# A fused attention and FFN layer on one core: a third PSUM bank for the projections, another order of GpSimd's work, and v turned by VectorE and a trip through DRAM

## The chip, the cores and the metric

The kernel runs on 1 core of one Trainium2 chip. The time is the device time of one execution in microseconds; a kernel's time is the median of its runs.

## The reference

The input has 2048 rows (8 sequences of 256 tokens) of 512 numbers. First attention with 32 heads of 128, grouped over 8 key/value heads, then a linear layer whose rows are switched on by clusters, each behind a layer norm and each added to its input:

```python
NH, NKV, D = (32, 8, 128)
qkv = layernorm(x) @ w_qkv                       # 512 -> 6144
scores = einsum('bqhgd,bkhd->bhgqk', q, k) * D ** -0.5
bias = where(rel >= 0, -slopes * sqrt(rel), -inf)  # causal
attn = softmax(scores + bias)
x = x + (attn @ v) @ w_o                         # 4096 -> 512
dots = softmax(layernorm(x) @ centroids.T / 0.1)
hits = dots > 0.01
dense = layernorm(x) @ weight.T + bias
x = x + where(any(hits, 1)[:, None] & any(hits, 0)[assignments], dense, 0)
```

## The kernel before

**Tiles and units.** The rows are cut into 4 quads of 512 tokens (two sequences each). A unit `u` of the main loop is one key/value head with its 4 query heads for one quad; there are 32 units, four quads for each of 8 head groups `g`. A unit does six projections (`project(u, i)`: k, then four heads of q, then v), the scores of 4 heads, a softmax, the product with v and the output product with w_o. It is pipelined over two units: in `body(u)` unit u is projected and scored while the probabilities of unit u-1 are applied to v (`apply_v`, six chunks) and pass through w_o (`project_out`, four tiles).

**Precision.** Every operand of TensorE is split in a high and a low float32r part, and a product is three matmuls (high·high, high·low, low·high: `three_pass`). So each result in PSUM is read twice: ScalarE copies it out as the high part, VectorE (or GpSimd, when the source lies in SBUF) writes what is left as the low part.

**Causal halves.** For the first 128 queries of a sequence (`qt == 0`) only 128 keys count. There `scores` multiplies the high part of q with the 256 columns `both` (k high and k low side by side), then the low part of q with the same 256 columns, and `add_bias` on VectorE adds the two halves.

**Turning.** The probabilities are turned for `apply_v` in two steps: VectorE turns 32x32 blocks into `ring_whole`, then SyncE's queue writes the chunk to the DRAM tensor `turned` and reads it back with the blocks rearranged (`turn_out`, `turn_in`). ScalarE makes `pT_hi` of it, GpSimd the low part (`pT_lo_part`, in place in `ring`). v is turned by TensorE: ScalarE copies the projection to `vT` in SBUF, TensorE transposes four 128x128 blocks (L1294), ScalarE writes `v_hi`, VectorE `v_lo`.

**Order.** Each engine's program is written out by hand, in order, with semaphores between the engines. The places that matter here:
- The projections alternate between the two PSUM banks `PJ`; project(u, i) waits until VectorE has read projection i-2 for its low part (`qk_lo_done`, L807 for q, L804 for k).
- GpSimd splits the next group's w_qkv at the end of every fourth unit (`split_qkv`, four chunks, each with the DMA issues of a later load behind it, `load_after`) and then opens `wqkv_ready`. It splits w_o in the second unit of a group between chunks of the probabilities (`split_o`, in `group`) and opens `wo_ready`, for which `project_out(u, 0)` waits.
- Units 0 to 3 also carry the layer norm of the next quad; units 30 and 31 the FFN's first work; what follows unit 31 is written out by hand.

## Time and profile before

| | |
|---|---|
| median of 3 runs | 1324.68 us (1323.49 to 1326.9) |
| the profiled execution, own time | 1328.74 us |
| its span in the trace | 1327.1 us |
| granted TensorE clock, mean over the span | 0.992 of full speed |
| busy: TensorE 96%, VectorE 72%, ScalarE 47%, GpSimd 36% | |

The span is the time from the first instruction in the trace to the last. A matmul's bar in the trace is longer than the distance to the next one, since matmuls overlap; how fast TensorE goes is read from the distance between starts.

### The profile page before, as it was taken

The numbers are of one execution on the slowest core, as the hardware profiler recorded it, in microseconds if no ns is written. First come the engines' busy times: TensorE is split into PE (matmuls) and PEld (weight loads), VectorE is DVE, ScalarE is ACT, GpSimd is POOL, SyncE is SP. The second block draws the span as 40 slices with busy tenths as digits, with TensorE's granted clock in tenths as the row PEclk, the third lists the DMA queues.
The fourth block names the chain that finished last, engine by engine and source line by source line (L and its number), as shares of the span: only waits on it lengthen the run. The fifth ranks groups of instructions, "written<-read, shape, count | busy, mean of one in ns | idle before, by whom it ended". The sixth has DMA issues, their size and how long they took to land.

```text
span 1327.1 us, 22073 instructions
## 1 busy us (share of the span) xinstructions
PE 1280.5 (96%) x6294; PEld 1068.1 (80%) x6294; DVE 952.6 (72%) x2800; ACT 619.5 (47%) x1675; POOL 477.7 (36%) x444
## 2 busy tenths in 40 slices
PE   8899999999999999999999999999999999999987
PEld 7688877888878887888878888888878888887875
DVE  7888666777666677776666677666666677678687
ACT  2655444544444445444444454444444544554433
POOL 4311625216242444215252353316252263224213
PEclk8899999999999999999999999999999999999989
DMA  5411334223232333323232343323232242312003
GB/s 181 147 63 62 106 97 134 95 93 105 79 103 79 107 121 123 102 76 111 77 104 95 100 129 103 100 81 98 84 126 95 95 134 82 120 48 96 26 23 127
DMA packets 140296, 130.34 MB, mean 98 GB/s; under 512 B 7920, under 2 KB 105712, under 8 KB 140272
## 3 DMA queue, kind: packets, MB, share of 16 engines
q1 hardware_dynamic: 134448, 111.70, 25.5%
q0 software_dynamic: 5824, 18.36, 4.7%
q8 instruction: 11, 0.18, 0.1%
q14 instruction: 13, 0.11, 0.0%
HBM read 76.28 MB, written 53.74 MB: 98 GB/s over the span
## 4 chain that ended last, share of the span: by engine, by line
PE 52%; issue 22%; POOL 15%; DVE 7%; ACT 1%; POOLq 1%; DMA 1%; DVEq 0%; SPq 0%; ACTq 0%
PE ps L1133 47%; POOL ring L480 5%; POOL wqkv_lo L441 3%; POOL wo_lo L441 2%; DVE prob L875 2%; POOL wqkv_hi L439 2%; DVE prob L862 1%; PE ps L1213 1%; PE ps L1212 1%; POOL wo_hi L439 1%; PE ps L1153 1%; POOL raw L450 1%; DVE ring_whole L825 1%; PE ps L1294 1%; POOL bias L494 0%
## 5 line engine op out<-in xcount | busy, mean ns | idle before, releaser
L1133 PE MATMUL ps<-xnT,wqkv_hi 128*128 (+1 forms) x1568 | 490.2, 394 | 13.6 <-DVE qT_lo L807 10.1
L480 POOL TENSOR_TENSOR ring<-ring_whole,pT_hi 128x512 fp32r<-128x512 f32 x189 | 244.9, 1296 | 704.0 <-ACT pT_hi L612 703.5
L623 ACT ACTIVATE prob<-prob,negmax 128x128 f32<-128x128 f32 (+1 forms) x512 | 229.0, 449 | 333.7 <-DVE negmax L862 328.9
L1133 PEld LDWEIGHTS ps<-xnT,wqkv_hi 128*128 128x128 f32 x1568 | 290.2, 188 | 85.1 <-DVE qT_lo L807 17.8
L1133 PE MATMUL ps<-xnT,wqkv_lo 128*128 (+1 forms) x784 | 306.0, 390 | 0.0
L1133 PE MATMUL ps<-wo_hi,oT_hi 128*128 128x512 f32 x512 | 204.4, 399 | 7.4 <-POOLq L506 7.4
L875 DVE TENSOR_SCALAR prob<-prob,rinv 128x128 f32<-128x128 f32 (+1 forms) x512 | 201.1, 435 | 9.1
L1133 PE MATMUL ps<-wo_lo,oT_hi 128*128 128x512 f32 x512 | 200.1, 391 | 0.0
L1133 PE MATMUL ps<-wo_hi,oT_lo 128*128 128x512 f32 x512 | 199.9, 390 | 0.0
L842 DVE TENSOR_TENSOR acc<-ps,acc 128x512 f32 (+1 forms) x128 | 86.7, 677 | 153.2 <-PE ps L1133 153.2
L1133 PEld LDWEIGHTS ps<-xnT,wqkv_lo 128*128 128x128 f32 x784 | 147.6, 188 | 31.5
L807 DVE SCALAR_TENSOR_TENSOR qT_lo<-ps,qT_hi 128x512 fp32r<-128x512 f32 x128 | 86.2, 673 | 112.9 <-ACT qT_hi L601 112.8
L612 ACT ACTIVATE pT_hi<-ring_whole 128x512 fp32r<-128x512 f32 x189 | 119.3, 631 | 91.5 <-DMA ring_whole<-turned 88.7
L601 ACT ACTIVATE qT_hi<-ps 128x512 fp32r<-128x512 f32 x128 | 76.4, 597 | 152.4 <-PE ps L1133 152.3
L825 DVE STREAM_TRANSPOSE ring_whole<-prob 128x512 f32<-128x512 f32 x189 | 130.1, 701 | 12.6
L1133 PEld LDWEIGHTS ps<-wo_hi,oT_hi 128*128 128x128 f32 x512 | 96.4, 188 | 27.1 <-POOLq L506 9.9
L1133 PEld LDWEIGHTS ps<-wo_hi,oT_lo 128*128 128x128 f32 x512 | 96.1, 188 | 21.5
L1133 PEld LDWEIGHTS ps<-wo_lo,oT_hi 128*128 128x128 f32 x512 | 96.6, 189 | 16.8
L1133 PE MATMUL ps<-kT,qT_hi 128*128 128x256 f32 x512 | 96.6, 286 | 2.4 <-DVE negmax L862 1.9
L836 DVE TENSOR_TENSOR oT_lo<-ps,oT_hi 128x512 fp32r<-128x512 f32 x128 | 87.9, 687 | 14.7 <-ACT oT_hi L616 14.7
L623 ACT ACTIVATION_READ_ACCUMULATOR prob<-prob,negmax 128x1 f32 x512 | 96.7, 189 | 0.0
L862 DVE CUSTOM_DVE_ANT_0 prob<-ps,bias 128x256 f32<-128x256 f32 x256 | 93.8, 419 | 2.0 <-DVE ring_whole L825 0.2
(128 smaller groups left out, 1758.3 us busy)
## 6 DMA issues: line engine op xcount, KB each, us to landing
turned<-ring_whole SPq DMA_DIRECT2D x189, 256.0 KB, 2.0
ring_whole<-turned SPq DMA_DIRECT2D x189, 256.0 KB, 2.9
raw<-in_L_attn_w_qkv POOLq DMA_DIRECT2D x28, 256.0 KB, 3.1
raw<-in_L_attn_w_o POOLq DMA_DIRECT2D x28, 256.0 KB, 3.2
raw<-in_L_attn_w_qkv POOLq DMA_DIRECT2D x28, 128.0 KB, 3.0
acc<-in_L_attn_hidden_states SPq DMA_DIRECT2D x3, 1024.0 KB, 8.2
out<-acc SPq DMA_DIRECT2D x3, 1024.0 KB, 4.3
acc<-in_L_attn_hidden_states SPq DMA_DIRECT2D x4, 256.0 KB, 4.0
```

Of the source, the lines that this page charges most:

```text
L441: pool.tensor_tensor(lo, source, hi.bitcast(F32), ALU.subtract).then_inc(raw_split, 1)
L480: pool.tensor_tensor(ring_slot(c), whole_slot(c), pT_hi[:, c % 2, :].bitcast(F32), ALU.subtract).then_inc(pT_lo_done, 1)
L601: ins = act.activation(qT_hi[:, i - 1, :], src, ACT.Copy, scale=SCALE)
L612: act.activation(pT_hi[:, c % 2, :], source, ACT.Copy).then_inc(pT_hi_done, 1)
L623: ins = act.activation(s, s, ACT.Exp, bias=negmax[:, n:n + 1], scale=-1.0, accum_out=rowsum[:, n:n + 1])
L807: ins = dve.scalar_tensor_tensor(qT_lo[:, i - 1, :], src, SCALE, qT_hi[:, i - 1, :].bitcast(F32), ALU.mult, ALU.subtract)
L825: dve.transpose(whole_slot(c).rearrange("p (j h c) -> p h j c", h=HPG, c=BLK), source.rearrange("p h (j c) -> p h j c", c=BLK)).then_inc(p ...
L836: dve.tensor_tensor(oT_view(u, oT_lo, k), pv_view(u, k), oT_view(u, oT_hi, k).bitcast(F32), ALU.subtract).then_inc(oT_lo_done, 1)
L842: dve.tensor_tensor(acc[:, at], ps[:, out_bank(u, k), :], acc[:, at], ALU.add).then_inc(added, 1)
L862: ins = dve.tensor_tensor_reduce(out=s, in0=ps[:, score_bank(u, i), bank_col:bank_col + (qt + 1) * P], in1=bias[:, h, :] if qt else s, sca ...
L875: ins = dve.tensor_scalar(s, s, rinv[:, n:n + 1], None, ALU.mult)
L1133: ins = pe.matmul(dst, l, r, start=start and m == 0, stop=stop and m == n - 1)
```

## The change

Seven things are done at once, and nothing of what is computed changes but one product that is left out because it is small (low part of q with low part of k, for `qt == 0` alone; elsewhere it never was computed).
1. Projections go round three PSUM banks (`proj_bank`: `PJ[0]`, `PJ[1]`, `TR[1]`), and project(u, i) waits for the low part of projection i-3.
2. v is turned by VectorE straight out of PSUM in 32x32 blocks into `vT`, then written to the new DRAM tensor `turned_v` and read back rearranged, on SyncE's queue; ScalarE writes `v_hi` from SBUF after `exps(u, 1)`, and GpSimd writes `v_lo` at the end of its unit (in the fourth unit of a group between the second and third chunk of w_qkv). TensorE's transposes of v, ScalarE's copy to `vT` and VectorE's `v_lo` are gone.
3. `split_qkv` issues its last two loads behind the last chunk, and TensorE waits for each chunk of w_qkv by itself.
4. In `group` the four w_o chunks start one chunk of probabilities earlier, and the loads behind the last two are issued after `wo_ready`.
5. For `qt == 0` the low part of q is multiplied with 128 columns instead of 256.
6. At the start GpSimd's first split waits for the layer norm (`ln_ready`); in unit 0 VectorE normalises and turns the first probabilities before `add_bias(0, 2)`.
7. Before unit 30 the weights of the FFN are turned through other banks, and in the tail `dense(1, 3)` moves ahead of `transpose_probs(u, 3)`.

In the code `sp` is SyncE, `pool` GpSimd, `act` ScalarE, `dve` VectorE and `pe` TensorE.

```diff
+        def proj_bank(u, i):
+
+            if is_first(u) and i == PROJ_OUTS - 1:
+                return PJ[0]
+            return (PJ[0], PJ[1], TR[1])[i % 3]
...
+            def turn_v(v):
+
+                sp.wait_ge(v_turned, v + 1)
+                sp.dma_start(turned_v, vT[:]).then_inc(v_out, 16)
+                sp.wait_ge(v_out, v * 16 + 16)
...
+                else:
+                    sp.dma_start(vT[:].rearrange("p (a x) -> p a x", a=P // BLK),
+                                 turned_v.rearrange("(a c) (b x) -> (c b) a x", a=P // BLK, b=P // BLK)).then_inc(v_in, 16)
...
             def split_qkv(g):
                 for c in range(NC):
+                    if c == 2:
+                        v_lo_part(g * QUADS - 1)
 
                     pool.wait_ge(raw_loaded[c % 2], g * 96 - 96 + 32 * (c // 2 + 1))
                     split(raw[:, c % 2, :], wqkv_hi[:, c, :], wqkv_lo[:, c, :], g * (2 * NC) + SETUP + c + 1)
-                    load_after(g, c)
-                pool.sem_inc(wqkv_ready, 1)
+                    if c < 2:
+                        load_after(g, c)
+                load_after(g, 2)
+                load_after(g, 3)
...
+            def v_lo_part(u):
+
+                pool.wait_ge(v_hi_done, u + 1)
+                pool.tensor_tensor(v_lo[:].rearrange("p t (a e) -> p a t e", a=P // BLK),
+                                   vT[:].rearrange("p (a t e) -> p a t e", a=P // BLK, t=TPQ),
+                                   v_hi[:].rearrange("p t (a e) -> p a t e", a=P // BLK).bitcast(F32),
+                                   ALU.subtract).then_inc(v_lo_done, 1)
...
+            pool.wait_ge(ln_ready, TPQ)
             for c in range(NC - 1):
...
-                    act.wait_ge(v_mm, u + 1)
-                    act.activation(v_hi[:], ps[:, TR[0], :].rearrange("p (t d) -> p t d", t=TPQ), ACT.Copy).then_inc(v_hi_done, 1)
+                    exps(u, 1)
+                    act.wait_ge(v_in, u * 16 + (16 + 16 * (P // BLK) if isinstance(u, int) and u == UNITS - 1 else 16))
+                    act.wait_ge(pv_mm, u * CHUNKS + CHUNKS)
+                    act.activation(v_hi[:].rearrange("p t (a e) -> p a t e", a=P // BLK),
+                                   vT[:].rearrange("p (a t e) -> p a t e", a=P // BLK, t=TPQ), ACT.Copy).then_inc(v_hi_done, 1)
                 if p is not None:
+                    act.wait_ge(v_lo_done, u + 1)
                     copy_logits(p)
...
+            def turn_v(u):
+
+                dve.wait_ge(qkv_mm, u * PROJ_OUTS + PROJ_OUTS)
+                dve.wait_ge(v_lo_done, u)
+                dve.transpose(vT[:].rearrange("p (b t e) -> p t b e", b=P // BLK, t=TPQ),
+                              ps[:, proj_bank(u, PROJ_OUTS - 1), :].rearrange("p (t b c) -> p t b c", t=TPQ, b=P // BLK)).then_inc(v_turned, 1)
...
-                if i == 0 and not first:
-                    pe.wait_ge(wqkv_ready, group_count(u))
...
+                    elif i == 0:
+                        pe.wait_ge(raw_split, (u >> 2) * (2 * NC) + c + 1)
...
-                        ins = pe.matmul(dst, q_lo, both, start=False, stop=True)
+                        ins = pe.matmul(dst[:, 0:P], q_lo, kT[:, 2 * b, 0, :], start=False, stop=True)
...
-                        else:
-                            pe.wait_ge(qk_lo_done, u * 5 + i - 1)
+                        elif i > 2:
+                            pe.wait_ge(qk_lo_done, 4 if is_first(u) and i == PROJ_OUTS - 1 else u * 5 + i - 2)
...
-                    pe.wait_ge(qkv_hi_done, u * PROJ_OUTS + 6)
-                    for t in range(TPQ):
-                        ins = pe.transpose(ps[:, TR[0], t * P:(t + 1) * P], vT[:, t * P:(t + 1) * P], ident[:])
-                    ins.then_inc(v_mm, 1)
+                    pe.wait_ge(v_turned, u + 1)
```

TensorE's program in the second half of a unit of the main loop; `qT_hi` and `qT_lo` are the weights, `kT` streams through. Before:

```order
L1212 MATMUL ps<-kT,qT_hi 128x256 [waits scores_biased]
L1213 MATMUL ps<-kT,qT_lo 128x256
L1212 MATMUL ps<-kT,qT_hi 128x256
L1213 MATMUL ps<-kT,qT_lo 128x256
L1133 MATMUL ps<-pT_hi,v_hi 128x512 [waits pT_lo_done]
L1133 MATMUL ps<-ring,v_hi 128x512
L1133 MATMUL ps<-pT_hi,v_lo 128x512
L1294 MATMUL ps<-ident,vT 128x128 [waits qkv_hi_done]
L1294 MATMUL ps<-ident,vT 128x128 x3
L1133 MATMUL ps<-wo_hi,oT_hi 128x512 [waits oT_lo_done]
```

The same place of the changed kernel:

```order
L1268 MATMUL ps<-kT,qT_hi 128x256 [waits scores_biased]
L1269 MATMUL ps<-kT,qT_lo 128x128
L1268 MATMUL ps<-kT,qT_hi 128x256
L1269 MATMUL ps<-kT,qT_lo 128x128
L1189 MATMUL ps<-pT_hi,v_hi 128x512 [waits pT_lo_done]
L1189 MATMUL ps<-ring,v_hi 128x512
L1189 MATMUL ps<-pT_hi,v_lo 128x512
L1189 MATMUL ps<-wo_hi,oT_hi 128x512 [waits oT_lo_done,v_turned]
```

The second product of each head writes 128 columns, the four transposes are gone, and the output product waits for VectorE's turn of v as well.

GpSimd's program in the second unit of a group (`L480`/`L514` is the low part of a chunk of probabilities, the rest splits w_o). Before, from the third of the four chunks of w_o on:

```order
L439 TENSOR_SCALAR wo_hi<-raw 128x512 [waits raw_loaded0]
L441 TENSOR_TENSOR wo_lo<-raw,wo_hi 128x512 [waits pool_step]
L454 REGISTER_ALU
L446 ISA [waits raw_split]
L446 DMA raw<-in_L_attn_w_qkv 128x512
L447 ISA
L447 DMA raw<-in_L_attn_w_qkv 128x2x128
L479 REGISTER_ALU
L480 TENSOR_TENSOR ring<-ring_whole,pT_hi 128x512 [waits pT_hi_done]
L439 TENSOR_SCALAR wo_hi<-raw 128x512 [waits raw_loaded1]
L441 TENSOR_TENSOR wo_lo<-raw,wo_hi 128x512 [waits pool_step]
L454 REGISTER_ALU
```

Now, from the same chunk on:

```order
L469 TENSOR_SCALAR wo_hi<-raw 128x512 [waits raw_loaded0]
L471 TENSOR_TENSOR wo_lo<-raw,wo_hi 128x512 [waits pool_step]
L513 REGISTER_ALU
L514 TENSOR_TENSOR ring<-ring_whole,pT_hi 128x512 [waits pT_hi_done]
L469 TENSOR_SCALAR wo_hi<-raw 128x512 [waits raw_loaded1]
L471 TENSOR_TENSOR wo_lo<-raw,wo_hi 128x512 [waits pool_step]
L513 REGISTER_ALU
L514 TENSOR_TENSOR ring<-ring_whole,pT_hi 128x512 [waits pT_hi_done]
L548 REGISTER_ALU
L513 REGISTER_ALU [waits raw_split]
L514 TENSOR_TENSOR ring<-ring_whole,pT_hi 128x512 [waits pT_hi_done]
L513 REGISTER_ALU
```

The DMA issues for the next w_qkv (L446, L447) stood between the third and the fourth chunk and behind the fourth; now both pairs stand behind the release (L548) and two chunks of probabilities more.

## Rows read from the trace of the kernel before

**Rows 1.** The page: busy us, share of the span and instructions of each engine
```profile
PE 1280.5 (96%) x6294; PEld 1068.1 (80%) x6294; DVE 952.6 (72%) x2800; ACT 619.5 (47%) x1675; POOL 477.7 (36%) x444
```

**Rows 2.** Waits, 60 to 1160 us: who waits, total us, times, longest
```profile
PE ps L1133 <- DVE qT_lo L807: 10.1, 11, 2.1
PE ps L1133 <- POOLq L506: 7.4, 6, 1.5
PEld ps L1133 <- DVE qT_lo L807: 17.8, 17, 2.5
PEld ps L1133 <- DVE kT L804: 8.0, 14, 0.8
```

**Rows 3.** Timeline, TensorE in the second unit of a group
```profile
671.00 0.39 PE L1133 MATMUL ps<-pT_hi,v_lo 128*128 128x512 f32 x1
672.37 0.74 PE L1133 MATMUL ps<-xnT,wqkv_hi 128*128 x2 [0.98 <-DVE qT_lo L807]
...
683.66 0.50 PE L1133 MATMUL ps<-wo_hi,oT_hi 128*128 128x512 f32 x1 [1.44 <-POOLq L506]
```

**Rows 4.** Timeline, GpSimd in the same unit
```profile
677.75 0.58 POOL L446 DMA_DIRECT2D raw<-in_L_attn_w_qkv  x1 [0.65 <-POOL wo_lo L441]
678.36 0.72 POOL L447 DMA_DIRECT2D raw<-in_L_attn_w_qkv  x1
...
681.07 1.28 POOL L441 TENSOR_TENSOR wo_lo<-raw,wo_hi 128x512 fp32r<-128x512 f32 x1
```

**Rows 5.** Timeline, TensorE: transposes of v, and 128x64 fp32 products
```profile
610.38 0.39 PE L1133 MATMUL ps<-pT_hi,v_lo 128*128 128x512 f32 x1
610.61 0.60 PE L1294 MATMUL ps<-ident,vT 128*128 128x128 f32 x4
610.96 0.48 PE L1133 MATMUL ps<-wo_hi,oT_hi 128*128 128x512 f32 x1
611.28 0.40 PE L1133 MATMUL ps<-wo_lo,oT_hi 128*128 128x512 f32 x1
...
1188.41 1.00 PE L1231 MATMUL ps<-fold,vT 128*128 128x64 f32 x8
1189.22 3.01 PE L1133 MATMUL ps<-xnT 128*128 128x512 f32 x12
```

**Rows 6.** Timeline, TensorE: scores of the first queries
```profile
609.19 0.28 PE L1212 MATMUL ps<-kT,qT_hi 128*128 128x256 f32 x1
609.31 0.28 PE L1213 MATMUL ps<-kT,qT_lo 128*128 128x256 f32 x1
```

**Rows 7.** Timeline, GpSimd's second half of splitting w_qkv, and VectorE beside it
```profile
616.47 1.85 POOL L441 TENSOR_TENSOR wqkv_lo<-raw,wqkv_hi 128x768 fp32r<-128x768 f32 x1
616.49 2.11 DVE L875 TENSOR_SCALAR prob<-prob,rinv 128x128 f32<-128x128 f32 x2
```

**Rows 8.** Timeline: one turn of probabilities, to ScalarE's copy, and ScalarE's next wait
```profile
619.31 0.71 DVE L825 STREAM_TRANSPOSE ring_whole<-prob 128x512 f32<-128x512 f32 x1
625.45 0.64 ACT L612 ACTIVATE pT_hi<-ring_whole 128x512 fp32r<-128x512 f32 x1 [1.86 <-DMA ring_whole<-turned]
...
615.69 0.51 ACT L623 ACTIVATE prob<-prob,negmax 128x256 f32<-128x256 f32 x1 [2.28 <-DVE negmax L862]
```

**Rows 9.** Timeline of the start: layer norm and GpSimd's first splits
```profile
10.13 4.57 DVE L792 TENSOR_SCALAR prob<-acc,meanvar,rs 128x512 f32<-128x512 f32 x3
10.21 3.75 POOL L441 TENSOR_TENSOR wqkv_lo<-raw,wqkv_hi 128x768 fp32r<-128x768 f32 x2 [6.82 <-ACT wqkv_hi L682]
```

**Rows 10.** Timeline, TensorE in unit 1
```profile
53.45 0.76 PE L1133 MATMUL ps<-pT_hi,v_hi 128*128 128x512 f32 x1 [3.05 <-POOL ring L480]
```

**Rows 11.** Busy time by window (us, engines, granted clock, DMA), unit 1
```profile
52.80:59.60 6.80, 5.33 (x12) 3.77 (x13) 6.39 (x20) 4.55 (x13) 2.25 (x3) 0.50 0.43 140
```

**Rows 12.** Timeline, TensorE: the tail
```profile
1263.55 0.63 PE L1176 MATMUL ps<-ident,prob 128*128 128x128 f32 x4 [2.10 <-DVE prob L875]
1266.12 0.79 PE L1133 MATMUL ps<-pT_hi,v_hi 128*128 128x512 f32 x1 [1.94 <-POOL ring L480]
```

More of the change, by code:

```diff
@@ L496, in group @@
                     pT_lo_part(u, c)
-                pT_lo_part(u + 1, 0)
+                v_lo_part(u)
                 pool.wait_ge(wo_mm, g * (4 * QUADS) + 4)
-                for h, after in enumerate(((1, 2), (3,), (4,), (5,))):
+                for h in range(HPG):
                     split_o(g, h)
-                    if h < 2 or not last:
+                    if h < 2:
                         load_after(g, NC + h)
-                    if h == HPG - 1:
-                        pool.wait_ge(raw_split, g * (2 * NC) + 2 * NC)
-                        pool.sem_inc(wo_ready, 1)
-                    for c in after:
-                        pT_lo_part(u + 1, c)
+                    pT_lo_part(u + 1, h)
+                pool.wait_ge(raw_split, g * (2 * NC) + 2 * NC)
+                pool.sem_inc(wo_ready, 1)
+                pT_lo_part(u + 1, 4)
+                pT_lo_part(u + 1, 5)
+                if not last:
+                    load_after(g, 2 * NC - 2)
+                    load_after(g, 2 * NC - 1)
+                v_lo_part(u + 1)
                 plain_body(u + 2)
                 if not last:
-                    plain_body(u + 3)
+                    for c in range(CHUNKS):
+                        pT_lo_part(u + 3, c)
                     pool.wait_ge(qkv_mm, (g + 1) * (PROJ_OUTS * QUADS))
@@ L541, in _ @@
             pool.sem_inc(wo_ready, 1)
-            for u in range(1, QUADS):
+            v_lo_part(0)
+            for u in range(1, QUADS - 1):
                 plain_body(u)
+            for c in range(CHUNKS):
+                pT_lo_part(QUADS - 1, c)
             pool.wait_ge(qkv_mm, PROJ_OUTS * QUADS)
@@ L651, in body @@
                 for i in range(PROJ_OUTS):
-                    if proj:
+                    if proj and i < PROJ_OUTS - 1:
                         proj_hi(u, i)
@@ L921, in body @@
                         proj_lo(u, i)
+                    if proj and i == PROJ_OUTS - 1:
+                        turn_v(u)
                     if attn:
@@ L959, in body @@
                     oT_lo_part(u, 3)
-                if proj:
-                    dve.wait_ge(v_hi_done, u + 1)
-                    dve.tensor_tensor(v_lo[:], ps[:, TR[0], :].rearrange("p (t d) -> p t d", t=TPQ),
-                                      v_hi[:].bitcast(F32), ALU.subtract).then_inc(v_lo_done, 1)
                 if attn:
@@ L969, in body @@
                     dense_part(p, source, 0)
+                if is_first(u):
+                    normalise(u, 0)
+                    normalise(u, 1)
+                    turn(u, 0)
                 if proj:
@@ L972, in body @@
                     add_bias(u, 3)
+                if proj and not is_first(u):
                     normalise(u, 0)
@@ L1364, in _ @@
             apply_v(u, 0)
+            pe.wait_ge(scores_biased, u * SCORE_BANKS)
+            dense(1, 3)
             pe.wait_ge(cl_exp_done, 3)
@@ L1367, in _ @@
             apply_v(u, 1)
-            pe.wait_ge(scores_biased, u * SCORE_BANKS)
-            dense(1, 3)
             apply_v(u, 2)
```

57 lines of the change are left out of this document (30 added, 27 removed).

## The prediction

> **What bounds the kernel now.** I read the page first: TensorE is busy for 96% of the span, the next engine for 72% [rows 1]. So two things count: what TensorE has to do, and where it waits. Its bars overlap, so I went to the timeline and took the distances between starts: 0.23 us from one 512-column matmul to the next (610.38 to 610.61 in [rows 5]) and 0.12 for 256 columns [rows 6]. Every larger distance is lost time. Then the waits between 60 and 1160 us [rows 2]: the matmul row waits 10.1 us in 11 places for VectorE's low part of q (L807), 7.4 in 6 places for L506, GpSimd's `wo_ready`; the weight loads wait 17.8 and 8.0 us for L807 and L804. These are two readings of the same stalls, and both err. Of the wait at 672.37 the bracket shows 0.98, but the starts are 1.37 apart, 1.14 more than the pace, since the bar before is 0.16 longer than the pace [rows 3]; another 0.11 follows it while weight loads catch up. Weight loads sit idle for a few hundredths anyway, so their sum is too high. The truth for the projections lies between 10.1 and 17.8 + 8.0 = 25.8.
>
> **The change, part by part.**
>
> *Transposes of v.* Four cost 0.35 us, and the matmul behind them comes 0.32 after its predecessor instead of 0.23 [rows 5]: 0.44 us a unit, 32 units, **14.1 us**, all on TensorE, so all on the path as long as nothing else is late. 14.1 is also the upper bound; the lower is 11.2 (0.35 alone).
>
> *128 columns instead of 256 for the low part of q.* 8 matmuls a unit, 256 in all, now 0.12 us each [rows 6]. No row shows a float32r product of 128 columns. On the one side, if only columns counted, 128 fewer would save half of what separates 512 from 256, (0.23 - 0.12) / 2 = 0.054 us each, 13.8 us in all. The nearest row is the 128x64 fp32 product: eight bars in 0.81 us, 0.10 each, though a quarter of the columns stream through [rows 5]; there the weight load sets the pace. A load goes with every one of these matmuls too, so I take about 0.11: 0.01 saved, **2.5 us**. On the other side, those eight bars belong to four instructions, so an fp32 product is 0.20; if the narrow float32r product went that way it would be 0.08 dearer, 20 us lost.
>
> The Trainium skill gives the column price: "TensorE: Matmul & The Clock Gate", section "Back-to-back issue gap", has 262 cycles for 256 columns and 134 for 128, about 53 ns less, which would make 13.7 us, and warns in the same place that this leaves out weight loads. By the one this term is 14, by the row 2.5; the row's kind of load stands before each of these matmuls, so I go by the row.
>
> *Third bank.* project(u, i) needs the low part of projection i-3, one projection and one `apply_v` (15 matmuls, 3.4 us) older. The longest wait is 2.5 us [rows 2], so nearly all of them go. Between 10.1 and 25.8; one recorded wait is worth its bracket plus 0.27, and counted by starts over the stretch, the 31 places where a projection waits make **21 us**. What hides VectorE's lateness after this is that 3.4 us; without it the 21 come back.
>
> *w_o earlier.* At 683.66 TensorE has waited 1.44 for the release (1.6 by starts) [rows 3]; GpSimd's last part of w_o ended at 682.35 and PE was ready at 682.07, the release itself costs the rest [rows 4]. Out of the way of the fourth chunk goes one pair of issues, 0.65 + 0.58 + 0.72 = 1.95 us, and behind it another, and the first split starts one chunk of probabilities (1.3 us) sooner. Added is one v_lo, 1.3 us, but it stands ahead of the unit's work in a long idle. So the release comes over 3 us earlier and the six waits go: 7.4 by brackets, + 6 x 0.27 = **9 us**. With the stalls ahead of it gone TensorE arrives 1.3 us earlier, still covered.
>
> *Start.* The layer norm's three VectorE operations take 4.57 us, and for 3.75 of them GpSimd's two splits run beside them [rows 9]; what is left when those end is 0.7 us, so most of the 4.57 is waiting. GpSimd now waits for the layer norm. What hangs on it comes up to 3.7 us earlier, GpSimd's splits about 2 later, and the first projection takes their chunks one by one as they come: **2.5 us**, between 0 and 3.
>
> *Unit 1.* TensorE waits 3.05 us at 53.45 [rows 10], and the granted clock of the 6.8 us around it is 0.50, that is 1.2 instead of 2.4 GHz [rows 11]: half of what TensorE does in them is lost, 2 to 3 us more. The first turn now comes two `add_bias` earlier; this shortens the wait to under 1, and I assume the clock stays at 2.4 GHz. GpSimd's v_lo of unit 0 stands before the same chunk, ready by then. **5 us**, 0 to 7.
>
> *FFN weights and tail.* One wait at 1156 (1.4) loses its cause, since the fourth tile goes to a bank that has long been free. In the tail two waits of 2.10 and 1.94 [rows 12] stand with 12 matmuls, `dense(1, 3)`, behind them; these now fill the first (2.7 us of work). I take 3, since VectorE works at the same time: **4.4 us** together, 1 to 7.
>
> *v's new way, a cost of nothing where it is covered.* VectorE's turn takes about 0.7 us as for probabilities [rows 8] and replaces a low part of about the same length; at 606 VectorE idles until `add_out`. Its price straight out of PSUM has no row; 0.7 to 1 us, hidden by 4 us of idle. Then two DMAs: from the start of a turn (619.31) to ScalarE's copy (625.45) it is 6.1 us [rows 8]. v's projection ends at 606, so `v_hi` can go at about 612.3; with `exps(u, 1)` moved ahead ScalarE comes to it at 612.9, and the next exponential is not asked for before 615.69 [rows 8]. So the trip may take 2.2 us longer before ScalarE's queue (the exponentials behind `v_hi`, hence VectorE's normalising, hence scores 4 to 7) is late. SyncE's queue holds only these two DMAs in that stretch. GpSimd's 32 v_lo (1.3 us) lie in its idle time, but for the one inside the w_qkv split. There VectorE's normalising already waits for GpSimd: two operations took 2.11 us, as long as GpSimd's 1.85 beside them, and end with it [rows 7]. Another such collision costs 1.3, 7 times. And in units 30 and 31 the logits wait for v_lo. For all these I subtract **4 us**.
>
> Sum: 14.1 + 2.5 + 21 + 9 + 2.5 + 5 + 4.4 - 4 = 54.5 us. The profiled execution took 1328.7 us (span 1327.1), 4.1 more than the median; so its like would be 1274, and the median **1270 us**.
>
> **The rivals.**
> *A, VectorE and GpSimd stay late (0.22).* At each of the seven changes of group GpSimd now works with fewer pauses, because DMA issues stand behind the last chunk and a v_lo among the chunks. Each normalising pair can wait up to 1.85 us [rows 7]. If half of the 30 us of waits stays and another 1.3 comes at each change: 15 + 9 = 24 less gain, 1294; milder forms lie down to 1276. For it: TensorE's waits sit exactly in the units with splits. Against: after the DMA issues are moved, VectorE's first pair falls on v_lo (1.3) instead of a w_qkv part (1.85). The Trainium skill states the cause ("SBUF — State Buffer", on the shared port pair: a VectorE operation in a two-port mode and a GpSimd operation lock each other out for the whole instruction); the trace agrees, with its 2.11 us beside 1.85.
> *B, columns alone set the narrow product (0.10).* 11 us more gain: 1259.
> *C, the narrow product goes the fp32 way (0.08).* 0.20 us each, 20 + 2.5 lost against my sum: 1293; the last price is the nearest row's, and the narrow product has never been seen here.
> *D, slower than before (0.04).* v's trip: from 2.2 us more than 6.1, each further microsecond delays ScalarE's exponentials in every unit. To lose all of 54.5 us in 32 units TensorE must wait 1.7 us a unit, with about 1.5 us of slack at the scores: a trip of 11.5 us or more. GpSimd's loads run beside it only in one unit of four, which speaks against. At 12 us it would be 16 more than that, 1341. The Trainium skill is on this side ("VectorE: DVE Perf Modes", "Rules for kernel authors": a 128x128 transpose belongs on TensorE if PSUM is a fit destination); the traces so far show the same detour working for probabilities, 6 chunks a unit.
>
> **How the numbers follow.** My case (0.56) gives 1270, by its bounds 1262 to 1280. B ends below, A and C above. From 1258 to 1292 lie nearly all of my case, B, and most of A: 8 in 10. Within 0.3% (4 us, about what a measurement of this kernel tells from no change) of 1324.7 nothing but a mixture of A, C and D lands: faster 0.95, same 0.02, slower 0.03.
>
> **What would show it.** In the trace after: no transposes of v; L1269 at a distance of about 0.11 us (B: 0.07; C: 0.20 or more); the distance of like starts over a group of four units smaller by 6 to 7 us; waits of TensorE for L807's successor near zero; `v_hi` waiting for its DMA under 0.5 us. The prediction is wrong if the wait for scores (negmax) grows where w_qkv is split, if a clock of 1.2 GHz comes up elsewhere, or if the narrow product shows another price.

## The result and the profile after

The changed kernel takes **1296.1 us** (median of 4 runs, 1294.1 to 1297.0) against 1324.5 for the kernel before; the ratio is 0.978 (95% interval 0.976 to 0.980). Forecast were 1270 us and a range of 1258 to 1292. The profiled execution has a span of 1295.3 us, 31.8 less than before; the sum of the prediction was 54.5 less.

First the page's busy times, where [rows 1] stood before:

```profile
PE 1253.9 (97%) x6166; PEld 1054.4 (81%) x6166; DVE 977.9 (75%) x2800; ACT 581.3 (45%) x1642; POOL 519.8 (40%) x476
```

Then TensorE's waits between 60 and 1160 us, to be read beside [rows 2]. The columns are us in all, times, and the longest.

```profile
PE ps L1189 <- DVE negmax L915: 10.5, 7, 1.6
PE ps L1189 <- DVE qT_lo L853: 3.6, 6, 0.6
```

The wait for GpSimd's release of w_o is gone and that for q's low part fell from 10.1 to 3.6. But the wait for `negmax` (VectorE's maxima, which free a score bank) at this line was 1.9 us in three places in the whole execution before, none of them in this stretch, and is now 10.5 in seven places. There are seven units in which GpSimd splits w_qkv.

The measure that has no overlapping bars is the distance between like matmuls of successive units. The first product of q with k in units 14, 15 and 16 stands in the kernel before at

```profile
572.32 0.28 PE L1212 MATMUL ps<-kT,qT_hi 128*128 128x256 f32 x1
...
608.96 0.28 PE L1212 MATMUL ps<-kT,qT_hi 128*128 128x256 f32 x1
...
647.13 0.28 PE L1212 MATMUL ps<-kT,qT_hi 128*128 128x256 f32 x1
```

and in the changed kernel at

```profile
555.49 0.28 PE L1268 MATMUL ps<-kT,qT_hi 128*128 128x256 f32 x1
...
591.57 0.28 PE L1268 MATMUL ps<-kT,qT_hi 128*128 128x256 f32 x1
591.68 0.22 PE L1269 MATMUL ps<-kT,qT_lo 128*128 128x128 f32 x1
591.74 0.34 PE L1268 MATMUL ps<-kT,qT_hi 128*128 128x256 f32 x1
591.91 0.22 PE L1269 MATMUL ps<-kT,qT_lo 128*128 128x128 f32 x1
591.98 0.34 PE L1268 MATMUL ps<-kT,qT_hi 128*128 128x256 f32 x1
...
629.90 0.28 PE L1268 MATMUL ps<-kT,qT_hi 128*128 128x256 f32 x1
```

Unit 14 (quiet) takes 36.64 us before and 36.08 after. Unit 15 (GpSimd's w_qkv split) takes 38.17 and 38.33: the pure work fell by 0.56 and the waiting grew by 0.72. Laid over the whole span, these distances give the sum that the prediction should have made:

| stretch | predicted | measured |
|---|---|---|
| work: transposes of v and narrow q_lo, 32 x 0.56 | 16.6 | 17.9 |
| waits in units 3 to 28 (third bank, w_o, v's new way: 21 + 9 - 4) | 26 | 9.6 |
| start and units 0 to 2, beside the work | 7.5 | 3.3 |
| unit 29 to the end, beside the work | 4.4 | 0.9 |

The last three rows come from the starts of units 3 and 29 (153.21 and 1139.11 us before, 148.22 and 1109.93 after) and the spans, less 0.56 a unit. One row is 16 us off. By the same distances, less those of quiet units, the seven units that follow a w_qkv split (the waits for w_o stood there) lost 21.0 us before and lose 5.5 now; the seven units with a w_qkv split lost 12.3 and now lose 18.1. In the first the change did most of what was forecast, in the second it made things worse.

What VectorE and GpSimd do in unit 15 after shows where. On VectorE the four scalings `prob<-prob,rinv` in pairs are the normalising that precedes a turn of probabilities. Before, the second pair of this unit, behind the one of [rows 7], found GpSimd idle and took 0.48 us:

```profile
618.71 0.48 DVE L875 TENSOR_SCALAR prob<-prob,rinv 128x128 f32<-128x128 f32 x2
```

After, VectorE has

```profile
598.59 1.74 DVE L928 TENSOR_SCALAR prob<-prob,rinv 128x128 f32<-128x128 f32 x1
...
598.59 1.93 DVE L928 TENSOR_SCALAR prob<-prob,rinv 128x128 f32<-128x128 f32 x2
...
600.63 1.68 DVE L928 TENSOR_SCALAR prob<-prob,rinv 128x128 f32<-128x128 f32 x1
...
600.63 2.47 DVE L928 TENSOR_SCALAR prob<-prob,rinv 128x128 f32<-128x128 f32 x2
```

(the rows of 598.59 and 600.63 stand twice, with the first operation and with both), and GpSimd

```profile
596.81 0.60 POOL L476 DMA_DIRECT2D raw<-in_L_attn_w_qkv  x1 [0.65 <-POOL wqkv_lo L471]
597.41 0.71 POOL L477 DMA_DIRECT2D raw<-in_L_attn_w_qkv  x1
598.14 1.30 POOL L520 TENSOR_TENSOR v_lo<-vT,v_hi 128x512 fp32r<-128x512 f32 x1
599.41 0.83 POOL L469 TENSOR_SCALAR wqkv_hi<-raw 128x768 fp32r<-128x768 f32 x1
600.33 1.89 POOL L471 TENSOR_TENSOR wqkv_lo<-raw,wqkv_hi 128x768 fp32r<-128x768 f32 x1
602.19 0.82 POOL L469 TENSOR_SCALAR wqkv_hi<-raw 128x768 fp32r<-128x768 f32 x1
603.10 1.83 POOL L471 TENSOR_TENSOR wqkv_lo<-raw,wqkv_hi 128x768 fp32r<-128x768 f32 x1
```

The first scaling alone lasts 1.74 us and ends at 600.33, with the break of 0.09 us between the third chunk's high and low part; the end of v_lo at 599.4, where the high part follows without a pause, did not let it in. Of the second pair, the first scaling lasts through the low part and ends at 602.31, 0.09 us behind it, though there too the next high part follows without a pause; the second scaling lasts through that high part, to 603.10. So each scaling can be held by a part of its own. Together 4.40 us where the kernel before had 2.11 + 0.48. The scores that need VectorE's next maxima then wait:

```profile
603.52 0.39 PE L1189 MATMUL ps<-wo_hi,oT_lo 128*128 128x512 f32 x1
605.51 0.38 PE L1189 MATMUL ps<-kT,qT_hi 128*128 128x256 f32 x1 [1.60 <-DVE negmax L915]
```

In two of the seven units the granted clock falls behind this wait, for 3.4 us:

```profile
65.00:68.40 3.40, 3.40 (x10) 2.63 (x10) 3.40 (x6) 0.60 (x1) 0.53 (x1) 0.50 0.00 0
310.80:314.20 3.40, 3.40 (x10) 2.73 (x9) 3.28 (x10) 0.76 (x3) 0.47 (x1) 0.50 0.75 264
754.50:757.90 3.40, 3.40 (x12) 2.82 (x11) 3.24 (x10) 1.00 (x3) 0.25 (x1) 0.50 0.77 278
```

(The columns are us, then busy time and count of PE, PEld, DVE, ACT and POOL; the next, 0.50, is the granted clock, the level 1.2 GHz. The first row belongs to unit 0, below.) The distances in units 7 and 19 are 39.91 and 39.84 us instead of 38.35: each of the two stretches costs 1.5.

### The profile page after: what moved, and what is told of

Read it like the earlier page. It is cut to its first block, busy times and chain, and to the rows that moved or that the text cites. A ratio compares the mean times of both kernels' runs of the same rounds, so it can differ in the third digit from the quotient of the medians.

```text
span 1295.3 us, 22145 instructions
## 1 busy us (share of the span) xinstructions
PE 1253.9 (97%) x6166; PEld 1054.4 (81%) x6166; DVE 977.9 (75%) x2800; ACT 581.3 (45%) x1642; POOL 519.8 (40%) x476
## 4 chain that ended last, share of the span: by engine, by line
PE 71%; DVE 18%; issue 7%; ACT 1%; POOL 1%; DMA 1%; DVEq 1%; SPq 0%; ACTq 0%; POOLq 0%
PE ps L1189 67%; DVE prob L928 6%; DVE prob L915 3%; PE ps L1268 2%; DVE ring_whole L878 1%; DVE prob L908 1%; PE ps L1209 1%; PE ps L1269 1%; DVE stats L799 1%; DVE rinv L924 1%; DVE qT_lo L853 1%; DVE negmax L915 1%; DVE selected L963 0%; DVE kT L850 0%; DMA acc<-in_L_attn_hidden_states 0%
## 5 line engine op out<-in xcount | busy, mean ns | idle before, releaser
L514 POOL TENSOR_TENSOR ring<-ring_whole,pT_hi 128x512 fp32r<-128x512 f32 x189 | 246.5, 1304 | 439.0 <-ACT pT_hi L655 438.5
L1189 PEld LDWEIGHTS ps<-xnT,wqkv_hi 128*128 128x128 f32 x1568 | 293.6, 189 | 68.7 <-DVE qT_lo L853 6.2
L928 DVE TENSOR_SCALAR prob<-prob,rinv 128x128 f32<-128x128 f32 (+1 forms) x512 | 226.1, 483 | 9.1
L520 POOL TENSOR_TENSOR v_lo<-vT,v_hi 128x512 fp32r<-128x512 f32 x32 | 41.5, 1298 | 188.3 <-ACT v_hi L716 188.2
L1189 PE MATMUL ps<-kT,qT_hi 128*128 128x256 f32 x512 | 96.9, 287 | 14.2 <-DVE negmax L915 13.7
L1189 PEld LDWEIGHTS ps<-kT,qT_hi 128*128 128x128 f32 x512 | 83.1, 191 | 23.8 <-DVE negmax L915 19.6
```

What stands on the lines that cost most here:

```text
L514: pool.tensor_tensor(ring_slot(c), whole_slot(c), pT_hi[:, c % 2, :].bitcast(F32), ALU.subtract).then_inc(pT_lo_done, 1)
L520: pool.tensor_tensor(v_lo[:].rearrange("p t (a e) -> p a t e", a=P // BLK), vT[:].rearrange("p (a t e) -> p a t e", a=P // BLK, t=TPQ), v_ ...
L928: ins = dve.tensor_scalar(s, s, rinv[:, n:n + 1], None, ALU.mult)
L1189: ins = pe.matmul(dst, l, r, start=start and m == 0, stop=stop and m == n - 1)
```

## The experiments

Differences are against the changed kernel's 1296.1. The kernel before, measured beside them, stood between 1324.3 and 1325.7.

| kernel | us | ratio to before (95%) |
|---|---|---|
| q_wide | 1297.7 | 0.979 (0.977 to 0.981) |
| v_lo_last | 1289.3 | 0.973 (0.971 to 0.974) |
| pauses_back | 1292.9 | 0.976 (0.974 to 0.978) |
| breaks | 1287.8 | 0.972 (0.970 to 0.974) |
| bank_only (on before) | 1317.4 | 0.994 (0.992 to 0.996) |
| two_banks | 1336.4 | 1.009 (1.007 to 1.011) |
| no_split | 1277.5 | 0.964 (0.962 to 0.965) |
| breaks_all_last | 1285.4 | 0.969 (0.968 to 0.971) |
| bank_and_order (on before) | 1316.1 | 0.993 (0.990 to 0.995) |
| unit0_old | 1295.9 | 0.977 (0.975 to 0.980) |
| tail_old | 1297.0 | 0.979 (0.977 to 0.980) |
| breaks_unit0 | 1283.2 | 0.968 (0.966 to 0.970) |
| pauses_last | 1291.4 | 0.975 (0.973 to 0.976) |
| order_breaks (on before) | 1304.5 | 0.985 (0.983 to 0.986) |
| best | 1291.9 | 0.975 (0.973 to 0.977) |
| best_halves | 1293.9 | 0.976 (0.974 to 0.978) |
| v_lo_behind_loads | 1291.1 | 0.974 (0.972 to 0.975) |
| one_chunk_halved | 1291.9 | 0.974 (0.972 to 0.977) |

### Is GpSimd what keeps VectorE late?

**no_split** leaves GpSimd's parts of w_qkv out for all groups but the first:

```diff
-                    split(raw[:, c % 2, :], wqkv_hi[:, c, :], wqkv_lo[:, c, :], ...)
+                    pool.sem_inc(pool_marks, 1); pool.sem_inc(pool_step, 1); pool.sem_inc(raw_split, 1)
```

> The changed kernel in which GpSimd leaves out the high and low parts of w_qkv for the groups 1 to 7 (the loads and every release stay, the weights in the matmuls are those of group 0; 28 x 2.7 us of GpSimd's work gone). It bounds from below what GpSimd's presence costs there. Theory P: the unit of the split falls from 38.35 us to about the 36.08 of a quiet unit, 7 x 2.3 + 3.2 for the clock = 19 us less, 1277; the 0.9 us one unit later, beside the w_o split, stay. Theory Q (VectorE's chain is too long by itself): no change.

18.6 us less, and the two largest waits of TensorE become

```profile
PE ps L1195 <- DVE qT_lo L859: 3.4, 6, 0.6
PE ps L1215 <- DVE prob L844: 2.0, 3, 0.9
```

The split units take 36.08 us, like quiet ones. So all of their waiting, the 18.1 us with the two clock stretches, hangs on GpSimd's split, and none on VectorE's own length of work.

**v_lo_last** moves v_lo behind the four chunks; **pauses_back** puts the loads for w_o back behind the third and fourth chunk; **breaks** only adds waits of GpSimd for itself:

```diff
# v_lo_last
                 for c in range(NC):
-                    if c == 2:
-                        v_lo_part(g * QUADS - 1)
...
+                v_lo_part(g * QUADS - 1)
                 load_after(g, 2)
# pauses_back
-                    if c < 2:
-                        load_after(g, c)
-                load_after(g, 2)
-                load_after(g, 3)
+                    load_after(g, c)
# breaks
                 if count is not None:
+                    pool.wait_ge(raw_split, count - SETUP - 1)
+                pool.sem_inc(pool_marks, 1)
...
                         v_lo_part(g * QUADS - 1)
+                        pool.wait_ge(v_lo_done, g * QUADS)
```

> The changed kernel with one step moved: in the unit in which GpSimd splits w_qkv, the low part of v stands behind the fourth chunk instead of ahead of the third. Theory P (GpSimd keeps VectorE out): in the changed kernel VectorE's two normalising pairs after 598.59 us took 1.93 and 2.47 us, 4.40 together where a quiet unit takes 0.96, and each ends only where GpSimd's stream of v_lo, chunk 3 high, chunk 3 low, chunk 4 high has a break of about 0.09 us, between a high and a low part. Without v_lo the first pair meets the break behind the high part almost at once, so the two take 2.7 to 3.0; TensorE's wait for negmax of 1.77 us in seven units shrinks to under 0.6, the two stretches at 1.2 GHz behind it go. Expected 8 to 16 us less than the changed kernel's 1296, so 1280 to 1288. Rival Q (VectorE's chain is simply too long in that unit once TensorE no longer waits for the projections, whatever GpSimd does): no change, 1296.

> The changed kernel with the loads for w_o issued again behind the third and the fourth chunk, as before, v_lo still ahead of the third chunk. Theory P: the first pair still waits 1.9 us (v_lo and the high part behind it), the second finds the idle 0.65 us that stands ahead of a load and takes 1.8 instead of 2.47; 0.65 a group less, 3 to 8 us with the clock, so 1288 to 1293. Rival Q: no change or 1 to 2 us more, since the fourth chunk is ready 1.2 us later.

> The changed kernel, same order, but GpSimd waits for the end of its own last operation before each high part of a split (and behind v_lo), which puts a break of about 0.09 us where it ran without one. It adds under 0.1 us to each of GpSimd's parts and takes no work away. Theory P: VectorE gets in at each break; the first pair ends at about 599.7 (1.1 us), the second takes at most one part more (0.9), 2 us together instead of 4.40, so the wait for negmax in seven units goes, with the two stretches at 1.2 GHz, and part of the 0.77 us wait one unit later, which stands beside the w_o split: 15 to 22 us less, 1274 to 1281. Rival Q: no change. Third way R (what matters is how much GpSimd works, not where it breaks): no change either, or slightly slower.

They gain 6.8, 3.3 and 8.3 us. All three are in the direction of theory P, and Q is out; v_lo_last and breaks stay short of what was written. Breaks takes no work off GpSimd: that it gains most shows that the pauses count, apart from the amount of work. Its pauses are not the 0.09 us of the expectation, but 0.31 behind v_lo and 0.20 ahead of the fourth chunk; the first pair now gets through behind v_lo, and the second meets only a high part:

```profile
593.95 1.34 DVE L930 TENSOR_SCALAR prob<-prob,rinv 128x128 f32<-128x128 f32 x2
...
595.40 1.00 DVE L930 TENSOR_SCALAR prob<-prob,rinv 128x128 f32<-128x128 f32 x2
```

```profile
595.31 0.82 POOL L471 TENSOR_SCALAR wqkv_hi<-raw 128x768 fp32r<-128x768 f32 x1 [0.31 <-POOL v_lo L522]
```

TensorE's wait for `negmax` at the scores is gone there, and six waits for `acc` (VectorE's sum of the outputs), 3.7 us in all, have come up, which the expectation did not have.

### What took the place of the waits that the third bank removed?

**bank_only** puts the third bank alone into the kernel before (`proj_bank` and the waits on `qk_lo_done` of the diff); **two_banks** takes it out of the changed kernel; **bank_and_order** is bank_only with GpSimd's new order, v the old way.

```diff
# bank_only, against before
-                src = ps[:, PJ[i % 2], :]
+                src = ps[:, proj_bank(u, i), :]
...
-                            pe.wait_ge(qk_lo_done, u * 5 + i - 1)
+                            pe.wait_ge(qk_lo_done, 4 if is_first(u) and i == PROJ_OUTS - 1 else u * 5 + i - 2)
# two_banks, against the changed kernel
-            return (PJ[0], PJ[1], TR[1])[i % 3]
+            return PJ[i % 2]
```

> The kernel before with the third bank alone: projection i goes to the banks PJ[0], PJ[1], TR[1] in turn and waits for the low part of projection i-3. The prediction's term: 21 us less than before's 1324, so 1303. Theory P (the waits of TensorE are VectorE's lateness beside GpSimd's splits, which comes back at the next place that needs VectorE, the scores): only what fits into slack is gained, 4 to 9 us, so 1315 to 1320, and the wait for negmax in the unit of the w_qkv split grows by 0.5 to 1.5 us.

> The changed kernel with two banks for the projections again, all else kept. The prediction's term: 21 us more than 1296, so 1317. Theory P: the wait moves from the scores back to the projections and costs little more in sum, 3 to 9 us, so 1299 to 1305; the waits for qT_lo grow by more than those for negmax shrink.

> The kernel before with the third bank and GpSimd's new order (releases of w_qkv chunk by chunk, loads behind the last two chunks, w_o with one chunk of the ring behind each part), but v still turned by TensorE and its low part on VectorE, so no v_lo on GpSimd; start, unit 0, the wide q_lo and the tail as before. By the prediction's terms 21 + 9 = 30 less than before, 1295. By the theory that part of VectorE's lateness comes back at the scores: TensorE keeps about 1.2 us in each unit of the w_qkv split and 0.9 in the next, as the changed kernel with v_lo last did, 15 of the 33 us lost in these units, so 18 less, 1306.

With the bank alone, 8.0 us are gained, not 21. The waits for q's low part are gone altogether, but not to the scores, as was expected. They are here:

```profile
PE ps L1139 <- POOLq L512: 18.6, 7, 3.1
PE ps L1355 <- DVE negmax L868: 1.3, 1, 1.3
```

TensorE comes earlier to w_o, which is no earlier: the wait for its release grows from 7.4 to 18.6 us. With GpSimd's new order on top this wait goes too, and the next one comes up:

```profile
PE ps L1142 <- DVE negmax L871: 12.9, 7, 2.0
```

So 1316.1 is only 1.3 less than with the bank alone, too little to tell from no gain, and both forecasts (1295 and 1306) are missed. There is no v_lo on GpSimd in this kernel, and yet VectorE's pairs are as late as in the changed one:

```profile
607.43 2.70 DVE L884 TENSOR_SCALAR prob<-prob,rinv 128x128 f32<-128x128 f32 x2
...
610.23 2.02 DVE L884 TENSOR_SCALAR prob<-prob,rinv 128x128 f32<-128x128 f32 x2
```

```profile
606.48 0.84 POOL L445 TENSOR_SCALAR wqkv_hi<-raw 128x768 fp32r<-128x768 f32 x1
607.41 1.84 POOL L447 TENSOR_TENSOR wqkv_lo<-raw,wqkv_hi 128x768 fp32r<-128x768 f32 x1
609.22 0.83 POOL L445 TENSOR_SCALAR wqkv_hi<-raw 128x768 fp32r<-128x768 f32 x1
610.13 1.84 POOL L447 TENSOR_TENSOR wqkv_lo<-raw,wqkv_hi 128x768 fp32r<-128x768 f32 x1
```

They take 2.70 + 2.02 us. In bank_only, where a load with its idle 0.65 us still stands between the low part and the next high part, the second pair gets in:

```profile
608.36 2.12 DVE L881 TENSOR_SCALAR prob<-prob,rinv 128x128 f32<-128x128 f32 x2
...
610.59 0.48 DVE L881 TENSOR_SCALAR prob<-prob,rinv 128x128 f32<-128x128 f32 x2
```

```profile
608.35 1.85 POOL L447 TENSOR_TENSOR wqkv_lo<-raw,wqkv_hi 128x768 fp32r<-128x768 f32 x1
610.85 0.60 POOL L456 DMA_DIRECT2D raw<-in_L_attn_w_o  x1 [0.65 <-POOL wqkv_lo L447]
```

The rows point at one edit of the new order, the two loads moved from between the chunks to behind them; in the changed kernel v_lo then adds a third part to the stream.

two_banks was missed by both theories: 40 us more. Its waits are

```profile
PE ps L1187 <- DVE qT_lo L851: 19.0, 9, 2.6
PE ps L1187 <- DVE negmax L913: 10.6, 7, 1.6
PE ps L1187 <- DVE kT L848: 8.1, 10, 1.1
```

and nine stretches at 1.2 GHz between 60 and 1140 us, 3.4 us each, cost about 15 (an estimate: half of each is lost). The wait for negmax stays as it is, so the two kinds of wait do not trade against each other here. The third bank is worth 8.0 us in the kernel before and 40.3 in the changed one: it has no price of its own that could be added up. Why kT's low part (10 waits) comes so late with two banks I have not taken apart.

**order_breaks** gives bank_and_order the breaks, **pauses_last** gives the changed kernel a load behind each chunk and v_lo behind all.

```diff
# pauses_last, against the changed kernel
-                    if c == 2:
-                        v_lo_part(g * QUADS - 1)
...
-                    if c < 2:
-                        load_after(g, c)
-                load_after(g, 2)
-                load_after(g, 3)
+                    load_after(g, c)
+                v_lo_part(g * QUADS - 1)
```

> The kernel before with third bank and GpSimd's new order, v the old way (1316.1), plus GpSimd's wait for its own last operation ahead of each chunk of w_qkv. Theory L: the second pair, 2.02 us there, gets in after one part, 2.7 of 4.72 us remain or less; the wait of 2.7 us a group at the scores falls to about 1: 9 to 13 us less, 1303 to 1307. Theory V: no v_lo here, so nothing to win, 1316.

> The changed kernel with a load behind each of the four chunks again, as before, and v_lo behind the last load. Theory L (the loads moved behind the chunks took away the idle 0.65 us in which VectorE's second pair got in; v_lo then adds to it): the pairs take 2.1 and 0.5 us as with the third bank alone, the unit of the split falls from 38.35 to about 36.6, the stretches at 1.2 GHz behind it go, 12 to 15 us less than 1296: 1281 to 1284. Theory V (v_lo among the chunks is the cause): no better than v_lo last alone, 1289.

order_breaks gains 11.5 us, as written, with no v_lo there: theory L holds for it. pauses_last gains only 4.7, near what theory V wrote (1289). The wait at the scores is gone, and another has come up at the next projection:

```profile
PE ps L1184 <- DVE acc L890: 8.0, 6, 1.4
```

TensorE waits for a sum into `acc`, which stands on VectorE behind the fourth pair. This pair comes after the fourth chunk's last part (it ends at 602.33) and ends behind v_lo in its new place:

```profile
602.85 2.21 DVE L923 TENSOR_SCALAR prob<-prob,rinv 128x256 f32<-128x256 f32 x2
```

```profile
603.61 1.30 POOL L515 TENSOR_TENSOR v_lo<-vT,v_hi 128x512 fp32r<-128x512 f32 x1
```

The first two pairs take 0.69 and 1.87 us, not the 2.1 and 0.5 of the expectation. So pauses_last moves two things at once, the pauses and v_lo, and does not settle by itself which of them counts. Lateness that is only pushed on in VectorE's queue is paid at the next place.

### The smaller terms

**q_wide** takes q_lo's product back to 256 columns, **unit0_old** and **tail_old** undo VectorE's order in unit 0 and `dense(1, 3)`'s place.

```diff
# q_wide
-                        ins = pe.matmul(dst[:, 0:P], q_lo, kT[:, 2 * b, 0, :], start=False, stop=True)
+                        ins = pe.matmul(dst, q_lo, both, start=False, stop=True)
# unit0_old
-                if is_first(u):
-                    normalise(u, 0)
-                    normalise(u, 1)
-                    turn(u, 0)
                 if proj:
                     add_bias(u, 2)
                     add_bias(u, 3)
-                if proj and not is_first(u):
# tail_old
+            apply_v(u, 1)
             pe.wait_ge(scores_biased, u * SCORE_BANKS)
             dense(1, 3)
```

> The changed kernel with the product of q_lo back at 256 columns. If TensorE were paced by columns, this costs 0.053 us x 256 = 13.7 us. By the trace of the changed kernel a pair of q_hi and q_lo takes 0.235 us with 128 columns as it did with 256 (0.239), only the split between the two changed (0.17 and 0.065), so no change: within 2 us of 1296. The prediction's term of 2.5 us would be 1298.6.

> The changed kernel with VectorE's old order in unit 0 (both further score pairs ahead of the first normalising). The prediction's term for unit 1: 5 us more, 1301. By the traces unit 1 gained 0.9 us beside the transposes and unit 0 nothing, since the 3.2 us wait of before came back as 2.2 at unit 0's scores, 1.1 and 1.0 at apply_v and a stretch at 1.2 GHz: between 2 us less and 2 us more than 1296.

> The changed kernel with dense(1, 3) back behind apply_v(31, 1). The prediction's term: 3 us more, 1299. By the traces the last stretch (from unit 31's scores on) became only 1.1 us shorter, 0.6 of it the transposes, since the chain of VectorE and ScalarE through exponentials, normalising and turn sets when the next chunk is there, whatever TensorE does meanwhile: 0 to 1 us more, 1296 to 1297.

q_wide is 1.6 us slower, inside both intervals; but in its trace a quiet unit takes 36.16 us instead of 36.08, 2.6 us over 32 units. unit0_old changes nothing that can be told (1295.9), and the 0.9 us of tail_old are too little to tell.

### A faster version

**breaks_all_last** has v_lo last and breaks in the w_o split too; **breaks_unit0** adds VectorE's old order in unit 0. **best**, **best_halves**, **v_lo_behind_loads** and **one_chunk_halved** try to go on from there, by loads between the chunks, low parts in halves, and v_lo behind the loads.

```diff
# breaks_all_last, in the w_o split, beside v_lo_last and breaks
+                    pool.wait_ge(raw_split, g * (2 * NC) + NC + h + 1)
+                    pool.sem_inc(pool_marks, 1)
                     pT_lo_part(u + 1, h)
+                    pool.wait_ge(pT_lo_done, u * CHUNKS + CHUNKS + h + 1)
# one_chunk_halved (best_halves: every chunk), in split, n = QKV_W // 2
+                    pool.tensor_tensor(lo[:, 0:n], source[:, 0:n], hi[:, 0:n].bitcast(F32), ALU.subtract).then_inc(half_split, 1)
+                    pool.wait_ge(half_split, half)
+                    pool.sem_inc(pool_marks, 1)
+                    lo, source, hi = lo[:, n:], source[:, n:], hi[:, n:]
```

> The changed kernel with v_lo behind the fourth chunk, and GpSimd waiting for the end of its own last operation ahead of each part of w_qkv and w_o and of the ring's parts between them. Theory P: both gains add in part, since v_lo no longer stands in VectorE's way and each pair waits for one part at most: against 1287.8 with breaks alone another 3 to 6 from v_lo, and 0.3 to 0.9 us a group at the projections beside the w_o split: 1277 to 1284. If GpSimd's amount of work is what counts, 1289 as with v_lo last alone.

> The kernel with all breaks and v_lo last (1285.4 in the call before), with VectorE's old order in unit 0: 2 us less to 2 us more than that.

> pauses_last plus the breaks of the w_qkv and w_o splits and VectorE's old order in unit 0. By theory L the two gains are of one cause in different places: 0.8 us a group less at the w_o split than pauses_last (as from 0.93 to 0.75 with the breaks) and 1 to 2 us at the start: 1277 to 1282.

> best, with each low part of w_qkv made in two halves of 384 columns with a break between them. What VectorE can be kept out for becomes 0.95 us instead of 1.85: the first pair, 2.1 us in pauses_last, takes about 1.2. TensorE's slack already covers part of it: 0 to 5 us less than best, if GpSimd's extra 0.2 us a chunk doesn't make the fourth chunk late.

> The fastest kernel so far (breaks everywhere, v_lo behind the fourth chunk, old order in unit 0: 1283.2) with v_lo also behind the two loads for w_o. In it VectorE's third and fourth pair took 0.83 and 0.68 us beside v_lo instead of 0.62 each. If what counts is a pair beside a part: 0.2 us a group, 1 to 2 us less, 1281.5 to 1282.5. If the length of GpSimd's stream counts: no change.

> The same, with the low part of the third chunk of w_qkv made in two halves of 384 columns and a break between them; the whole part (1.89 us) kept VectorE's second pair out for 1.86 us where 0.48 is its own time. If a pair beside a part counts: that pair takes 0.9 to 1.0, 0.9 us a group at the scores and next to nothing later, 3 to 6 us less than the kernel beside it: 1277 to 1280. If the length of GpSimd's stream counts (one more operation, 0.2 us more): 0 to 1.5 us more.

breaks_all_last (1285.4) comes out 1.4 above its range. breaks_unit0 is the fastest, 1283.2 us, 12.9 less than the changed kernel. Its first two pairs in the split unit:

```profile
591.49 0.77 DVE L931 TENSOR_SCALAR prob<-prob,rinv 128x128 f32<-128x128 f32 x2
...
592.36 1.87 DVE L931 TENSOR_SCALAR prob<-prob,rinv 128x128 f32<-128x128 f32 x2
```

The second still sits through one low part of 1.89 us. The four attempts to go on came out at 1291 to 1294, 8 to 11 us slower, which none of the expectations had. All four have one thing in common: v_lo stands behind the last load. v_lo_behind_loads changes nothing else against breaks_unit0 and is 7.9 us slower by itself, so the place of v_lo accounts for nearly all of the loss. There it is the third pair that meets v_lo, and TensorE's wait for `acc` is back:

```profile
602.10 2.14 DVE L931 TENSOR_SCALAR prob<-prob,rinv 128x256 f32<-128x256 f32 x2
```

```profile
602.51 1.30 POOL L520 TENSOR_TENSOR v_lo<-vT,v_hi 128x512 fp32r<-128x512 f32 x1
```

```profile
PE ps L1187 <- DVE acc L898: 7.1, 6, 1.2
```

In one_chunk_halved and best_halves the second pair does get shorter (1.04 and 1.03 us). Unit 11 is then 37.45 us long in one_chunk_halved against 38.03 in v_lo_behind_loads, but unit 15 is 38.67, since a later pair there takes 3.40 us, and the medians (1291.9 and 1291.1) show no gain. Halves, or loads between the chunks, with v_lo left behind the fourth chunk were not tried, so this section does not show that they fail. What it shows is that about a part's length of lateness in each split unit depends on how the two queues fall against each other to a few tenths of a microsecond.

## Why the prediction was wrong

- **The work on TensorE was right.** 14.1 + 2.5 us were forecast, 17.9 measured. Narrow q_lo alone is 2.6 by the units' distance; the row of 128x64 products was the right one to go by. The rest, 36.64 less q_wide's 36.16 in 32 units, is 15.4 for the transposes, somewhat above what was called their upper bound. The trace differs in one thing: a pair of q_hi and q_lo takes 0.24 us as before (591.74 to 591.98 above), and it is q_lo that passes in 0.07 while q_hi takes 0.17. So the distance behind L1269 is the 0.07 that was to tell of rival B, and B is wrong all the same: the distance of one matmul was no safe sign, that of the pair would have been. The Trainium skill's column price ("TensorE: Matmul & The Clock Gate", "Back-to-back issue gap") would have made 13.7, an estimate; the measured 2.6 does not agree with it.
- **The step that failed is the third bank's, "these 21 us go", with w_o's 9 and the minus 4 for v's new way.** I added up where TensorE waited and took each wait as removed by the edit that removes its semaphore. But the waits hang together: bank_only took away the one for q's low part and the one for w_o grew to 18.6 us; bank_and_order took that away and the scores wait 12.9. "Where a stall goes, say what is late next": I named w_o and claimed that it stays covered, and did not follow VectorE's queue to the scores of the unit with the w_qkv split. Of 33.3 us of waiting in units 3 to 28 (their 985.9 us less 26 x 36.64) 23.6 are left, 18.1 of them in the seven units with a w_qkv split, which had 12.3.
- **The argument against rival A was wrong.** It said that VectorE's first pair would fall on v_lo (1.3) instead of a low part (1.85). A pair is two scalings, and each can be held by a part of its own; the first scaling of the first pair was even held over two parts, v_lo and the high part behind it. The pairs took 1.93 and 2.47 us. The prediction named 1.3 for each of seven groups, 9.1 in all, and took off 4 for this and everything else of v's new way; the two pairs alone lost 1.8 each time, the clock came on top, and moving v_lo gave 6.8 back. Rival A deserved more than 0.22: its condition, fewer pauses on GpSimd, was in the order of instructions, and its price in [rows 7]. That its sum, 1294, comes so near to 1296.1 is in part luck: 16.4 us were lost in A's way, and most of the rest in the start and the tail, of which A says nothing.
- **Unit 1: 5 forecast, nothing that can be told from 0 measured** (unit0_old). The wait of [rows 10] came back in parts: TensorE waits 2.07 us at unit 0's scores and 0.98 and 0.88 at apply_v, and has 3.4 us at 1.2 GHz at 65.0.
- **The start stays open.** Unit 0's scores begin at 35.31 us instead of 37.82, just the 2.5 of the forecast. But no run undoes the start alone, and bank_only, with the old one, begins them at 36.69, while breaks_all_last, with the new one, has 36.31: part of the 2.5 may be the difference between any two executions.
- **Tail: 4.4 forecast, 0.9 measured.** dense(1, 3) fills a wait, but the chunks of the ring come when GpSimd has them: TensorE waits 0.97 and 2.27 us for them at 1235 and 1238. Units 30 and 31 lost 0.4 each at the logits, behind v_hi and v_lo.
- **The trip of v through DRAM was priced rightly, at nothing for TensorE.** Quiet units, and with no_split the split units too, take 36.08 us. v_hi waits 11.6 us for its DMA in 8 places, more than the 0.5 each that I wrote. What cost something is v_lo's place in GpSimd's stream. From bank_and_order to the changed kernel, which is v's way with the narrow q_lo and the small terms, 20 us are gained.

## What to carry to other kernels

Waits at several places of one unit of work may be one engine's lateness; when the nearest is removed, ask what is the next thing that TensorE needs from the same queue, until the queue itself has caught up. Where two engines keep each other out, look at the pauses in the stream of one and at what stands in the other's queue at that moment: an instruction that looks like mere overhead (a DMA issue with its wait) may be the door. A wait of an engine for its own last operation is a cheap experiment for this, and here part of the fastest version. And when several attempts fail alike, look first for the edit that they share.

## What the runs showed of the hardware

A scaling of probabilities on VectorE (`TENSOR_SCALAR`; a pair takes 0.48 us alone) that meets a GpSimd part ends about 0.09 us behind it: the one of 600.63 at 602.31, the low part beside it at 602.22. The gap of 0.09 us between a high part and its low part let in the scaling that waited (to 600.33) and the next one (to 600.52). The gap of 0.31 us behind v_lo, in breaks, let in both of the first pair. Where one GpSimd part follows the other without a gap it goes either way: in the changed kernel the scaling that waited for a low part got in ahead of the next high part in all seven groups, and the one that met v_lo was passed over in six, and lasted 1.74 us. What decides between the two, no run shows. The Trainium skill ("SBUF — State Buffer", "Who interferes with whom") has the lock for the length of one instruction. The scaling of 600.63 agrees with that; the one of 598.59, passed over at 599.41, was held for longer.

TensorE's clock fell to 1.2 GHz for 3.4 us behind two of six waits of equal length (1.60 us by the brackets, in units 7 to 27), in q_wide behind two others (at 607.2 and 904.2, waits of 1.55), and in v_lo_last not behind one of 2.70 us at 161.5. So two executions of nearly the same program differ by 1.5 us in a unit, and the clock cannot be read off the wait alone.
